# A fused transformer stack with sorted experts: ranking, sort and indirect writes of each half placed earlier

## What is computed

```python
x = x + attn_rope(layernorm(x))
x = x + ffn(layernorm(x))
x = x + attn_cov(layernorm(x))
x = x + ffn(layernorm(x))

def ffn(x):                               # the part that the change touches
    h = x + attention(layer_norm(x))      # 16 heads of 8
    t = layer_norm(h).reshape(B * T, D)
    probs = softmax(t @ w_gate)           # 8 experts
    tw, ti = top_k(probs, 2)
    tw = tw / sum(tw)
    for e in range(8):
        we = sum(where(ti == e, tw, 0))
        out += we[:, None] * (gelu(t @ w1[e] + b1[e]) @ w2[e] + b2[e])
    return h + out
```

## Time and profile before

| | us |
|---|---|
| median of 3 runs (lowest, highest) | 901.11 (899.53, 1022.9) |
| span of the profiled execution | 896.4 |
| TensorE busy | 767.0 (86%) |
| VectorE busy | 544.5 (61%) |
| ScalarE busy | 543.4 (61%) |
| GpSimd busy | 484.2 (54%) |

### The profile page before, as it was taken

How to read it: one execution, slowest core, us unless ns; L and a number is a source line. 1 busy time by engine, 2 the same in 40 slices (tenths; PEclk the granted TensorE clock), 3 DMA queues, 4 the chain that set the end, 5 groups by cost and what they waited for, 6 DMA issues and landing times.

```text
span 896.4 us, 21301 instructions
## 1 busy us (share of the span) xinstructions
PE 767.0 (86%) x7166; PEld 546.7 (61%) x7166; DVE 544.5 (61%) x1370; ACT 543.4 (61%) x1264; POOL 484.2 (54%) x906
## 2 busy tenths in 40 slices
PE   1999999999999399697988999999999948968970
PEld 1756655666565189497964565566666525958970
DVE  4699899788988123012486887878889822211232
ACT  0377777878787256154546676787877834715640
POOL 6667678747762621504645665844777273060436
PEclk9999999999999789698999899999999977978995
DMA  9300000000000436266210000000000042635842
GB/s 274 111 3 3 3 2 3 4 3 3 4 2 4 130 107 175 79 182 175 79 38 13 16 18 5 4 3 3 3 3 3 3 124 77 173 103 143 245 124 67
DMA packets 57657, 56.29 MB, mean 63 GB/s; under 512 B 6856, under 2 KB 42448, under 8 KB 57552
## 3 DMA queue, kind: packets, MB, share of 16 engines
q1 hardware_dynamic: 39200, 39.13, 15.5%
q0 software_dynamic: 4096, 8.40, 3.2%
q10 hardware_dynamic: 14256, 7.41, 2.9%
HBM read 40.10 MB, written 14.29 MB: 61 GB/s over the span
## 4 chain that ended last, share of the span: by engine, by line
PE 56%; DVE 21%; issue 11%; POOL 7%; DMA 3%; ACT 2%; another core or an unknown queue 0%; ACTq 0%; POOLq 0%; DVEq 0%; SPq 0%
DVE M L1109 11%; PE bankO L466 11%; PE bankR L720 8%; PE bankE L707 7%; PE bankE L485 7%; PE bankE L439 6%; DVE QKV L1071 2%; POOL Yg L1578 2%; PE bankR L452 2%; PE bankE L476 2%; PE bankR L506 2%; PE bankR L536 1%; PE bankR L738 1%; PE bankR L554 1%; DMA Yg<-sorted_y,SLOT 1%
## 5 line engine op out<-in xcount | busy, mean ns | idle before, releaser
L1109 DVE TENSOR_REDUCE M<-bankR 128x2 f32<-128x512 f32 x512 | 326.4, 684 | 62.7 <-PE bankR L452 56.9
L834 ACT ACTIVATE Pr<-bankE 128x512 f32<-128x512 f32 x512 | 277.7, 595 | 129.5 <-PE bankE L439 109.1
L466 PE MATMUL bankO<-Pr,Vx 128*32 128x256 f32 x2048 | 170.5, 406 | 18.8 <-issue 16.1
L452 PE MATMUL bankR<-KQ 32*128 32x256 f32 x1024 | 171.3, 339 | 5.0 <-DVE M L1109 2.9
L439 PEld LDWEIGHTS bankE<-KQ 32*128 32x128 f32 x1024 | 79.6, 188 | 97.1 <-issue 64.2
L439 PE MATMUL bankE<-KQ 32*128 32x256 f32 x1024 | 133.3, 335 | 0.5 <-issue 0.5
L1312 DVE COPY Yb<-bankR 128x128 f32<-128x128 f32 x92 | 26.4, 290 | 167.9 <-PE bankR L720 111.1
L452 PEld LDWEIGHTS bankR<-KQ 32*128 32x128 f32 x1024 | 110.1, 191 | 17.1 <-DVE M L1109 12.8
L951 ACT ACTIVATE G<-bankE,W 128x128 f32<-128x128 f32 x368 | 101.5, 384 | 24.8 <-PE bankE L707 14.0
L707 PE MATMUL bankE<-XTT,W 128*128 128x128 f32 x736 | 105.1, 288 | 11.4 <-issue 4.6
L1578 POOL DMA_INDIRECT Yg<-sorted_y,SLOT x64 | 62.2, 971 | 95.6 <-DMA sorted_y<-Yb 42.0
(11 more groups left out here) (169 smaller groups left out, 1147.0 us busy)
## 6 DMA issues: line engine op xcount, KB each, us to landing
W<-in_w1b SPq DMA_DIRECT2D x92, 258.0 KB
sorted_y<-Yb ACTq DMA_DIRECT2D x92, 64.0 KB
XT<-sorted_u SPq DMA_DIRECT2D x20, 256.0 KB
sorted_u<-Yg SPq DMA_DIRECT2D x2, 1472.0 KB, 9.7
KQ<-MT SPq DMA_DIRECT2D x128, 4.0 KB
X<-in_x SPq DMA_DIRECT2D x8, 128.0 KB, 7.3
sorted_u<-U,SLOT POOLq DMA_INDIRECT x64
Yg<-sorted_y,SLOT POOLq DMA_INDIRECT x64
```

Of the source, the lines that this page charges most:

```text
L452: k = mm(dve_bank("raw", layer, b, h)[:, z * T:z * T + T], QT[rows, kb, g, z * P:z * P + P], KT[rows, kb, g, :], start=True, stop=True)
L466: k = mm(bankO[SL * j:SL * j + SL, cols], Vx[:, b % VB, kc, HG * g + j, :], Pr[:, g % 2, j, kc, :], start=(g % 2 == 0 and kc == 0), stop=( ...
L834: nc.scalar.activation(Pr[:, (h // HG) % 2, h % HG], act_bank("S", layer, b, h).rearrange("p (k q) -> p k q", k=TT), ACT.Exp, scale=EXP_SC ...
L1109: v.tensor_reduce(M[:, b % 2, :, h], dve_bank("raw", layer, b, h).rearrange("p (t k) -> p t k", t=TT), AX.X, ALU.max, negate=True).then_in ...
```

## The change

Three things are placed elsewhere; no instruction is added or taken away.

- In a step, `do_uT` goes from behind raw product 3 to behind raw product 1, `do_gate` and `choose` go up by two maxima, and `weigh` runs in the same step, behind maxima 6, instead of in the next one (`gone` is dropped).
- The ranking and the sort of the first half go from the end of step 17 and from step 18 into step 17 (`ranking(a)` is true where `a` is batch 6), and GpSimd's `scatter(ph, 0)` goes from behind step 18 to behind step 17.
- In `drain`, the gating of batches 6 and 7 goes from tiles 1, 4, 6 and 8 to tiles 0 to 3, ranking and sort of the second half from tiles 9 and 10 to 4 and 5.

```diff
+        def ranking(a):
+            return a and LAYERS[a[0]] == "ffn" and a[1] == NB - 2
...
@@ TensorE, step
                 if a:
                     do_mT(*a, 1)
-                if a and LAYERS[a[0]] == "ffn" and a[1] == NB - 1:
-                    do_rank(a[0] // 2, 0, 1)
+                if ranking(a):
+                    do_rank(a[0] // 2, 0, 0)
...
                 if m:
                     do_raw(*m, 1)
+                if ranking(a):
+                    do_rank(a[0] // 2, 0, 1)
+                if u:
+                    do_uT(*u)
                 if a:
                     do_pv(*a, 0, 0)
...
                 if m:
                     do_raw(*m, 3)
                 if u:
-                    do_uT(*u)
+                    do_gate(*u)
...
                     do_raw(*m, 5)
-                if u:
-                    do_gate(*u)
...
@@ TensorE, drain
+                if i == 0:
+                    do_uT(layer, NB - 2)
                 if i == 1:
-                    do_uT(layer, NB - 2)
-                if i == 4:
                     do_gate(layer, NB - 2)
                     do_uT(layer, NB - 1)
-                if i == 6:
+                if i == 2:
                     do_gate(layer, NB - 1)
-                if i == 9:
+                if i == 4:
                     do_rank(ph, 1, 0)
-                if i == 10:
+                if i == 5:
                     do_rank(ph, 1, 1)
...
-                    if s == STEPS - DRAIN - 2:
-                        do_rank(ph, 0, 0)
...
@@ ScalarE, step
                     do_exp(*a, 2)
+                if u:
+                    do_uT(*u)
+                if a:
                     do_exp(*a, 3)
                     do_exp(*a, 4)
-                if u:
-                    do_uT(*u)
...
                     do_exp(*a, 6)
+                if block_of(u) is not None:
+                    do_gate_exp(*block_of(u))
...
@@ VectorE, step
-            def step(gone, u, t, a, m, n, p, nxt):
+            def step(u, t, a, m, n, p, nxt):
                 if a:
                     do_max(*a, 7)
-                if a and LAYERS[a[0]] == "ffn" and a[1] == NB - 1:
-                    sort_rows(a[0] // 2, 0)
                 if m:
                     do_max(*m, 0)
+                if ranking(a):
+                    copy_totals(a[0] // 2, 0)
...
                 if m:
                     do_max(*m, 1)
+                if ranking(a):
+                    sort_rows(a[0] // 2, 0)
...
+                if u:
+                    do_gate(*u)
                 if m:
                     do_max(*m, 4)
+                if block_of(u) is not None:
+                    choose(*block_of(u))
...
-                if u:
-                    do_gate(*u)
-                if block_of(gone) is not None:
-                    weigh(*block_of(gone))
-                if block_of(u) is not None:
-                    choose(*block_of(u))
                 if m:
                     do_max(*m, 6)
+                if block_of(u) is not None:
+                    weigh(*block_of(u))
...
@@ VectorE, drain
-                if i == 4:
+                if i == 1:
                     do_gate(layer, NB - 2)
-                if i == 6:
+                if i == 2:
                     do_gate(layer, NB - 1)
                     choose(ph, 3)
-                if i == 8:
+                if i == 3:
                     weigh(ph, 3)
-                if i == 9:
+                if i == 4:
                     copy_totals(ph, 1)
-                if i == 10:
+                if i == 5:
                     sort_rows(ph, 1)
...
             def mixture(ph):
-                weigh(ph, 2)
...
@@ GpSimd
-                    if s == STEPS - DRAIN - 1:
+                    if s == STEPS - DRAIN - 2:
                         scatter(ph, 0)
```

More of the change, by code:

```diff
@@ L894, in step @@
                     do_exp(*a, 2)
-                    do_exp(*a, 3)
-                    do_exp(*a, 4)
                 if u:
@@ L899, in step @@
                 if a:
+                    do_exp(*a, 3)
+                    do_exp(*a, 4)
                     do_exp(*a, 5)
@@ L917, in step @@
                     do_exp(*a, 7)
-                if block_of(u) is not None:
-                    do_gate_exp(*block_of(u))
                 if n and LAYERS[n[0]] == "rope":
@@ L1384, in _ @@
                         norm_in(0, 0)
-                    step(sequences(ph, s - 1)[0], *sequences(ph, s), sequences(ph, s + 1)[5])
-                    if s == STEPS - DRAIN - 2:
-                        copy_totals(ph, 0)
+                    step(*sequences(ph, s), sequences(ph, s + 1)[5])
                 mixture(ph)
```

## The result

The changed kernel takes 916.46 us (median of 4 runs, 909.42 to 924.82) beside 900.75 of the kernel before (median of 4): a ratio of 1.0167, with a 95% interval of 1.0111 to 1.0223. That is 15.7 us more where 10 were predicted, inside the range and on the predicted side of no gain; whether the loss passes 2% is not settled by the interval.

A forecast was written before the change was run, and what follows sets the result against it. TensorE bounds full steps, VectorE step 17; the large holes lie beside GpSimd's indirect writes. Terms 0.5 + 3.0 + 0.9 + 0.6 give +5.0 us a phase, +10 for two: 911 us, range 897 to 924.

The forecast's parts named there:

- gating in the steps: Steps 14, 16, 18: later U delays TensorE's transposition by 0 to 1.2 us a phase; 0.5 taken.
- sort: step 17: Step 17, which waits for VectorE, gets the first half's sort: +3.8 us a phase, +3.2 to +5.0.
- credit in step 18: Step 18: with the sort gone, divide starts sooner; -0.8 us a phase, 0 if TensorE didn't wait for it.
- writes earlier, standstill with them: First half's sixteen writes end about 301 instead of 312 us, TensorE's hole moves too: +0.9 us, 0 to +3.4.
- weight loads: Before the experts: start about 308 instead of 293.3 us, rows there about when TensorE asks; 0 us, 3 if not.
- second half sooner: Drain: the second half's gating, sort and writes come some tiles earlier; +0.6 us a phase, 0 to +3.
- the standstill comes along: Steps 17 and 18: TensorE slow beside the moved writes, 284.5 to 303.5 us; about 18 us with 20 to 28 matmuls.
- Rival A: TensorE's hole doesn't follow the writes; waiting for batch 5's U still prevents a gain; about 903 us, chance 0.18.
- the cap: First half: batch 5's U, behind the sixteenth write, comes at 304.5; experts not before 321.7 us, so no gain.
- zero over the pair: Attention steps: moving weigh delays the even step by 1.1 us and shortens the odd one by 1.1.
- the refilling term: Behind TensorE's hole in steps 17 and 18, three engines must fill their pipeline again: 0.5 us, 0 to 3.
- Rival B: More is lost in dense steps 17 and 18: 12.2 us a phase, 925 us, deciding from 9 a phase; chance 0.20.

The follow-up runs named there:

- experiment 5: Kernel before with only the new gating places in the attention steps; sort, writes and drain as before: 910.06 us beside 896.28, ratio 1.0154.
- experiment 3: Changed kernel with the first half's sixteen writes put back behind step 18, the sort still in step 17: 920.92 us, ratio 1.0265.
- experiment 2: Changed kernel with the old drain, so only the first half's changes: 918.18 us beside 896.14, ratio 1.0234.
- experiment 1: Kernel before with only the new order of drain: 897.49 us beside 896.14, ratio 1.0002.
- experiment 7: Changed kernel with the old gating, only the weights of batches 2 and 3 moved to the head of step 17: 914.87 us, ratio 1.0192.
- experiment 12: Changed kernel with one pause for landing, behind the 8th write of the second half: 872.76 us beside 862.35 on the third chip, ratio 1.0118.
- experiment 10: Kernel of experiment 7, first half's writes split behind steps 17 and 18, landing pauses after each four in all runs: 850.30 us, 0.9885 of 859.36.
- experiment 6: Kernel of experiment 1 with the second half's writes in four groups of four, one every three tiles: 868.60 us beside 896.28, ratio 0.9674.
- experiment 9: Kernel before with GpSimd waiting for landing behind the 4th, 8th and 12th write of each run: 882.52 us beside 859.36, ratio 1.0246.
- 8: Kernel of experiment 7, first half's writes in four groups among the steps, second half's one a tile: 866.67 us beside 896.28, ratio 0.9668.

## Why the prediction was right, and where it wasn't

The terms of a phase, the predicted ones beside those that the experiments give. The measured ones are half the difference of two medians, each taken against the kernel before on its own chip (896.14 and 896.28 us), and hold to 2 or 3 us:

| term | predicted us | measured us | by |
|---|---|---|---|
| gating in the steps | +0.5 | +6.9, of which 4.5 in steps 13 to 16 | experiment 5 |
| sort: step 17, credit in step 18 and the tail | +3.8 - 0.8 | +5.5, of which 2.4 in step 17 | experiment 3 less 5 |
| writes earlier, standstill with them | +0.9 | -1.4, not clear of noise | experiment 2 less 3 |
| weight loads | 0 | 0, not waited for | trace |
| second half sooner | +0.6 | 0.1 (-0.9 to +1.0) | experiment 1 |
| a phase | +5.0 | 11.0; 7.9 in the first comparison | experiment 2; result |

The split depends on the order in which the parts are added. Sort and writes without the new gating cost 9.3 us a phase (experiment 7, which has the new `drain` too), and with them in place the gating adds only 1.7. That the time fell inside the range owes something to luck: the two dearest terms were too small by 6.4 and 2.5 us, and on the chip of experiment 2 the first half alone costs twice the 10 us of the forecast.

**Right: the standstill comes along.** 36 matmuls in 16.5 us, from some 7 us behind the first write to 3 behind the last. I had said 20 to 28 in 18. Rival A, by which it would stay away, fell there. The rule behind it (the Trainium skill, SBUF — State Buffer, "SBUF: two separate sides": a transfer can't slow compute) doesn't cover what the traces of two chips show, 22 matmuls in 16.5 us beside sixteen writes in a row against 209 in 24.4 with pauses; the third chip's trace agrees with it, 121 in 14.3. By what way the writes hold TensorE's results back the traces don't show. One rival that they speak to is that TensorE's code is loaded too late beside the writes. The profile lists the transfers that load instructions: none lands from 288 to 314 us in the changed kernel. But none lands from 288 to 304 in experiment 12 either, where TensorE works on until 296, and in experiment 1 one lands at 355, inside a standstill that lasts until 367. That speaks against this rival.

**Right: the cap.** The prediction reckoned that batch 5's U comes at 304.5, behind the writes, and that the first half can't win for that reason alone. In the changed kernel the standstill covers it, since VectorE's statistics are late too; GpSimd and then TensorE:

```profile
307.27 0.23 POOL L1405 TENSOR_SCALAR lnsmall<-meanvar 128x2 f32<-128x2 f32 x1 [5.40 <-DVE meanvar L1043]
```

```profile
310.88 0.69 PE L568 MATMUL bankE<-ident,U 128*128 128x128 f32 x2
```

In experiment 12, without a standstill, TensorE transposes it at 304.57, the predicted moment, after 8.6 us of waiting. Its part II is 51.5 us, with this as its longest wait. The cap belongs to GpSimd's order and not to the early sort: in experiment 10 batch 5 is normalised between the eighth and the ninth write, and the first expert transposition comes at 312.29.

**Right in its place, too high in size: the sort in step 17.** It runs from 279.09 to 282.20 in the changed kernel, where the earlier trace rows had 288.64 to 292.30, between maxima that TensorE's products wait for:

```profile
279.09 0.17 DVE L1277 TENSOR_SCALAR ntiles<-bankR 128x8 f32<-128x8 f32 x1 [0.22 <-PE bankR L693]
...
282.02 0.18 DVE L1303 TENSOR_SCALAR EID<-npast 128x23 uint32<-128x23 f32 x1
```

The step took 17.02 us in experiment 3 for 13.27 before, but 14.58 in experiment 5 without the sort: 1.3 of the 3.75 us come with the gating and 2.4 with the sort. That the sum hits the predicted 3.8 is luck. The credit in step 18 didn't show: of the 5.5 us that the sort costs in all, some 3 lie behind step 17.

**Right: weight loads later, not waited for.** SyncE issues them at 312.47 instead of 293.31, 4 us behind the predicted 308, and the rows at 319.62; the first transposition at 331.77 waits for neither:

```profile
312.47 7.10 SPq L399 DMA_DIRECT2D W<-in_w1b  x7
319.62 13.69 SPq L388 DMA_DIRECT2D XT<-sorted_u  x4
```

**Wrong: "zero over the pair".** This is the step that failed. I moved `weigh` from an odd step to an even one and let the two cancel, as if each step were as long as VectorE's work. They are as long as TensorE's: before, it is busy 15.8 of 16.1 us. Taking a microsecond from VectorE in a step that TensorE bounds gives nothing, adding one at the end of the even step holds the last banks of maxima. And the gate product, two raw products sooner, takes its bank of the ring of three right behind the one that `divide` must empty. Both waits stand in TensorE's timeline of the changed kernel, where before had neither at these places:

```profile
240.17 0.50 PE L456 MATMUL bankR<-KQ 32*128 32x256 f32 x2 [0.54 <-DVE M L1113]
...
264.11 0.58 PE L577 MATMUL bankR<-w_gate,UT 128*128 128x8 f32 x4 [0.38 <-DVE On L1127]
```

Steps 13 to 16 take 16.75, 17.74, 16.73 and 17.75 us (16.04 to 16.19 before). The named waits (0.54 once and 0.38 twice in two steps) come to 1.3 of the 2.3 us that a pair of steps lost; what each of the moved pieces costs by itself was not tried. The prediction had looked at the bank ring for the sort (the three score banks are no cushion) and not for the gate product.

**Mis-sized: the refilling term,** "0.5 us (0 to 3)" for the engines behind the standstill, and the granted clock with it. The old hole had 7.6 us of work behind it before the experts; the new one has most of step 18 and the tail, and runs it mostly at the lower level. Between the end of the standstill and the first expert transposition the changed kernel has

```profile
304.80:331.80 27.00, 26.23 (x165) 13.72 (x166) 9.66 (x44) 13.34 (x28) 5.93 (x14) 0.59 0.32 89
```

165 matmuls in 27.0 us, busy throughout, at 0.59. Rival B had this mechanism and asked for 9 us a phase; the medians give 8 in the first comparison and 11 in experiment 2, so the truth lies on the line between forecast and B. The reason that it held against B, that the old hole too was followed by work at that clock, was true and weighed the wrong thing: by these traces what counts is how much work follows.

## What to carry to other kernels

Before counting a moved piece as neutral, ask which engine bounds the step that it leaves and the step that it enters, and which ring of banks its result now takes a place in; a balance within one engine's work says nothing where another one sets the step. Where an engine shows late results with no releaser beside a row of GpSimd's indirect DMAs, cut the row: pauses of 1.7 us after every fourth write, placed where nothing waits for the last one, were worth 28 us of 896 (experiment 6). Measure such a remedy on more than one chip: on the one without the standstill, pauses in all four runs, two of which the experts wait for, cost 23 us (experiment 9).

## What the runs showed of the hardware

- Sixteen indirect writes issued every 1.27 us stop TensorE for some 16 to 19 us in the first comparison and on two chips behind it, and don't on a third, where the kernel before is 37 us faster (859 to 896). By what way the writes do it is open, why one chip has it and another not, and whether it is the chip or its state at that time. How many writes in a row start it was not settled: four don't (experiment 6), and in the changed kernel the chain of waits breaks at 288.80, during the sixth.
- The dearest part of the loss goes with a granted clock at the lower level: the same stretch of program, 313 matmuls, was 32.2 us busy at a mean of 0.82 and 48.6 us at 0.59 (experiment 7), while the time in which TensorE wasn't busy fell from 16.4 to 10.3 us.
- The losses of two parts of the change don't add: 13.8 and 18.6 us alone, 22 for both.
- Neither of the two best kernels, 8 and 10, was run on both kinds of chip, and the second half of 6 was not joined with the first half of 8; the best that is shown is 866.7 to 896.3 on the one kind and 850.3 to 859.4 on the other.
